# A fused ViT block: the slot experts in two batches, started four steps earlier, with constant products on TensorE

## The reference

```
p = patches(x)                          # 32 x 36 x 768
h = LN(LN(p) @ W_proj)                  # tokenizer, two layer norms with gains
q, k, v = h @ W_qkv ; q, k normalized over the tokens of an image
attn = softmax(q^T k * temp)            # per image and head, 24 x 24
h = LN(h + (attn v) @ W_proj + b_proj)
# slot experts: 8 experts x 4 slots
logits = unit(h) @ unit(slots) * scale  # per token 32 logits
D = softmax over tokens ; C = softmax over slots
X~ = D^T unit(h)                        # 32 slots x 192 per image
H  = gelu(X~[expert] @ W_down + b_down) # 24 values per slot
Y~ = H @ W_up[expert] + b_up            # 192 values per slot
h = LN(h + C Y~)
```

## Time and profile before

| | us |
|---|---|
| median of 3 runs | 141.82 (139.89 to 144.46) |
| profiled execution | 140.0 |
| its span | 138.0 |
| PE / DVE / ACT / POOL busy | 115.0 / 88.9 / 69.0 / 67.0 |
| mean granted TensorE clock | 0.939 |

### The profile page before, as it was taken

How to read it: one execution, slowest core, us unless ns; L and a number is a source line. 1 busy time by engine, 2 the same in 40 slices (tenths; PEclk the granted TensorE clock), 3 DMA queues, 4 the chain that set the end, 5 groups by cost and what they waited for, 6 DMA issues and landing times.

```text
span 138.0 us, 4819 instructions
## 1 busy us (share of the span) xinstructions
PE 115.0 (83%) x1779; PEld 93.6 (68%) x1779; DVE 88.9 (64%) x380; ACT 69.0 (50%) x234; POOL 67.0 (49%) x158
## 2 busy tenths in 40 slices
PE   0297799999699999999999999997986860999920
PEld 0297799888377868578787796866964630788700
DVE  0211999999643687985857558586987440159980
ACT  3000004242862848648675686846644468763553
POOL 8500277767847428837265382743664000007871
PEclk9999999999999999999999999999999555599995
DMA  1999899988000000000000000000000000000232
GB/s 14 337 293 278 269 305 320 314 319 214 5 7 0 5 0 7 5 0 7 0 5 5 0 5 0 10 5 0 5 0 7 0 0 0 5 0 24 72 89 71
DMA packets 7677, 10.34 MB, mean 75 GB/s; under 512 B 2056, under 2 KB 5032, under 8 KB 7656
## 3 DMA queue, kind: packets, MB, share of 16 engines
q1 hardware_dynamic: 7656, 10.06, 24.2%
HBM read 9.17 MB, written 0.88 MB: 73 GB/s over the span
## 4 chain that ended last, share of the span: by engine, by line
PE 47%; DVE 22%; issue 12%; POOL 10%; ACT 4%; DMA 3%; SPq 1%; POOLq 1%; DVEq 0%; ACTq 0%
DVE st L649 8%; PE ps L565 7%; PE ps L436 6%; PE ps L476 5%; PE ps L496 3%; PE ps L542 3%; PE ps L399 3%; DMA wt<-in_w_tok 3%; PE ps L489 3%; PE ps L519 3%; DVE y L663 3%; PE ps L578 3%; DVE st L671 2%; PE ps L507 2%; PE ps L407 2%
## 5 line engine op out<-in xcount | busy, mean ns | idle before, releaser
L417 PE MATMUL ps<-wc,xT 128*108 128x192 f32 (+1 forms) x132 | 23.0, 327 | 1.5 <-DVE wc L637 1.5
L940 ACT ACTIVATE hT<-ps,b,g 96x108 f32<-96x108 f32 (+1 forms) x22 | 8.4, 430 | 27.9 <-PE ps L426 27.9
L417 PEld LDWEIGHTS ps<-wc,xT 128*108 128x108 f32 (+1 forms) x132 | 20.7, 170 | 2.0 <-DVE wc L637 1.8
L436 PE MATMUL ps<-wqk,hT 96*108 96x384 f32 (+1 forms) x44 | 16.2, 490 | 0.7 <-ACT qp L962 0.7
L1125 POOL TENSOR_SCALAR pw<-mv 108x1 f32<-108x1 f32 (+1 forms) x11 | 3.7, 337 | 21.3 <-DVE mv L780 21.3
L476 PE MATMUL ps<-hT,wv 96*128 96x108 f32 (+1 forms) x88 | 12.5, 284 | 0.0
L1139 POOL TENSOR_SCALAR var<-mv 108x1 f32<-108x1 f32 (+1 forms) x11 | 2.4, 223 | 18.9 <-DVE mv L875 18.4
L950 ACT ACTIVATE sq<-ps 108x384 f32<-108x384 f32 (+1 forms) x11 | 5.4, 490 | 12.4 <-PE ps L436 12.4
L476 PEld LDWEIGHTS ps<-hT,wv 96*128 96x128 f32 x88 | 10.7, 191 | 0.7
L649 DVE BATCH_NORM_STATS2 st<-xs 108x6 f32<-108x384 f32 (+1 forms) x22 | 10.9, 540 | 0.2 <-issue 0.2
L960 ACT ACTIVATE km<-ps,imgsel 108x192 f32<-108x192 f32 (+1 forms) x32 | 11.0, 418 | 0.0
(11 more groups left out here) (106 smaller groups left out, 304.6 us busy)
## 6 DMA issues: line engine op xcount, KB each, us to landing
xT<-in_x_t SPq DMA_DIRECT2D x10, 324.0 KB, 7.0
xs<-in_x SPq DMA_DIRECT2D x10, 324.0 KB
out<-o SPq DMA_DIRECT2D x10, 81.0 KB
wt<-in_w_tok SPq DMA_DIRECT2D x1, 576.0 KB, 4.2
wqk<-in_w_qk SPq DMA_DIRECT2D x1, 288.0 KB, 8.7
xT<-in_x_t SPq DMA_DIRECT2D x1, 216.0 KB, 7.5
xs<-in_x SPq DMA_DIRECT2D x1, 216.0 KB
wv<-in_w_v SPq DMA_DIRECT2D x1, 192.0 KB, 9.0
```

The lines of the kernel that those rows point to most:

```text
L417: mm = pe.matmul(tokp(g), xT[:, o + kc * n:o + (kc + 1) * n], wc[:, kc, :], start=kc == 0, stop=kc == KC - 1)
L436: mm = pe.matmul(qkp(g), hT[:, f, t0:t0 + tokens(g)], wqk[:, f, :, :, :].rearrange("p j h d -> p (j h d)"), start=f == 0, stop=f == 1)
L940: ins = act.activation(hT[:, f, t0:t0 + tokens(g)], htp(g)[:, f, :], ACT.Identity, bias=b2[:, f:f + 1], scale=g2[:, f:f + 1])
```

## The change

- `hidden` works on two batches, groups 0 to 5 (18 images) and 6 to 10 (14 images). `w_down` and `w_up` are padded to 32 values per expert, so that each expert has 32 partitions, and pairs of experts lie side by side (`j = n // 2`). `gelu(b)` is two activations over all 128 partitions. `wu` comes in one load.
- In place of `slot_out`: `widen(b)` multiplies each expert's weights with its slots only, for the whole batch, 16 products that give the outputs with the 192 values on partitions (2 x 96) and the slots along the row; `take_lower` (ScalarE) and `take_upper` (VectorE) copy halves of them to SBUF; `turn_u(g)` turns a group back by the identity; `take_y(g)` copies it (ScalarE). The bias is a product of its own in `combine(g)`.
- hidden(0), gelu(0) and widen(0) run in step 12; turn_u and combine of groups 0 to 5 in steps 13 to 16 and behind them; the second batch after the last step.
- `keep_busy(count, bank)` multiplies a constant 128 x 128 tile with itself into a bank that is free then: 11 ahead of `offset`, 3 behind `column_means`, 2 in step 11, 3 or more in each step from 12 on, 9 around widen(1).

```diff
-HB = ((0, 4), (4, 8), (8, NG))
+HB = ((0, 6), (6, NG))
+HS = 12
+WIDE = {13: (0,), 14: (1, 2), 15: (3,), 16: (4, 5)}
...
-            sp.wait_ge(cleared, 6)
-            for j in range(4):
-                sp.dma_start(wu[32 * j:32 * j + HID, :, :], w_up[j]).then_inc(experts_in, 16)
+            sp.dma_start(wu[:, :, :].rearrange("p e d -> p (e d)"), w_up).then_inc(experts_in, 16)
...
+            def keep_busy(count, bank):
+                for _ in range(count):
+                    pe.matmul(ps[:, bank, 0:128], steady[:, :], steady[:, :], start=True, stop=True)
...
                 for n in range(NE):
-                    j = n % 4
+                    j = n // 2
                     for f in range(2):
-                        mm = pe.matmul(hp(b, i1 - i0)[32 * j:32 * j + HID, n // 4, :, :], wd[:, f, n, :],
+                        mm = pe.matmul(hp(b, i1 - i0)[32 * j:32 * j + 32, n % 2, :], wd[:, f, n, :],
                                        xt[:, f, i0:i1, n, :], start=f == 0, stop=f == 1,
                                        tile_position=(0, 32 * j))
...
+            def widen(b):
+                i0, i1 = batch(b)
+                pe.wait_ge(hb_ready, b + 1)
...
+                for e in range(2):
+                    for f in range(2):
+                        for j in range(4):
+                            r = slice(32 * j, 32 * j + 32)
+                            mm = pe.matmul(utp(i1 - i0)[:, j, f, :, e, :], wu[r, e, f * F:(f + 1) * F],
+                                           hb[r, e, 0:(i1 - i0) * NP], start=True, stop=True,
+                                           tile_position=(32 * j, 0))
+                mm.then_inc(utp_ready, 1)
...
+            def turn_u(g):
...
+                for f in range(2):
+                    u = widened(b)[:, f, i0:i0 + images(g), :, :]
+                    mm = pe.transpose(ytp(g)[:, f * F:(f + 1) * F],
+                                      u.rearrange("p i j s -> p (i j s)"), ident[0:F, 0:F])
+                mm.then_inc(ytp_ready, 1)
 
             def combine(g):
...
+                pe.matmul(yop(g), cT[0:sl, g, 0:n], bu[0:sl, :], start=True, stop=False)
+                pe.wait_ge(yt_ready, g + 1)
+                pe.matmul(yop(g), cT[0:sl, g, 0:n], yt[0:sl, g % NQ, :], start=False, stop=True).then_inc(yop_ready, 1)
+
+            pe.wait_ge(steady_set, 1)
+            keep_busy(11, 3)
             offset()
             column_means()
+            keep_busy(3, 3)
...
                 at(logits, s - 5)
+                if s == HS:
+                    pe.wait_ge(experts_in, 16 * (3 + 1))
+                    hidden(0)
...
                 at(mix, s - 2)
+                if s == HS - 1:
+                    keep_busy(2, 0)
+                if s == HS + 1:
+                    keep_busy(3, 5)
+                if s == HS + 2:
+                    keep_busy(3, 5)
+                if s > HS + 2:
+                    keep_busy(3, 5)
                 at(turn_xn, s - 4)
+                if s == HS:
+                    keep_busy(4, 2)
+                if s == HS + 2:
+                    keep_busy(3, 4)
                 at(slot_in, s - 6)
                 at(norms, s)
+                if s == HS:
+                    widen(0)
+                for g in wide(s - 1):
+                    combine(g)
+                for g in wide(s):
+                    turn_u(g)
+            combine(4)
+            hidden(1)
+            combine(5)
+            keep_busy(6, 5)
+            widen(1)
+            keep_busy(3, 5)
+            turn_u(6)
+            for g in range(7, NG):
+                turn_u(g)
+                combine(g - 1)
             combine(NG - 1)
```

(The waits of the keep_busy lines on the last reader of their bank are left out here.) VectorE does take_upper(0) at the end of step 12, and last_residual, last_stats and last_moments of the groups of `WIDE` one step after their turn_u, last_shift two steps after it; then take_upper(1) and groups 6 to 10. ScalarE:

```diff
             for s in range(17):
                 at(exp_e, s - 2)
                 at(take_v, s - 2)
+                if s == HS:
+                    act.wait_ge(experts_in, 16 * (3 + 1))
+                    gelu(0)
                 at(square, s)
                 at(take_c, s - 6)
...
                 at(exp_c, s - 5)
...
                 at(take_slots, s - 6)
-                if s == NG + 4:
-                    act.wait_ge(experts_in, 16 * (3 + 4))
-                    gelu(0)
+                if s == HS:
+                    take_lower(0)
+                for g in wide(s):
+                    take_y(g)
+                for g in wide(s - 3):
+                    last_norm(g)
+            last_norm(1)
+            last_norm(2)
             gelu(1)
-            gelu(2)
-            for g in range(NG):
+            take_lower(1)
+            take_y(6)
+            take_y(7)
+            last_norm(3)
+            take_y(8)
+            last_norm(4)
+            take_y(9)
+            last_norm(5)
+            take_y(10)
+            last_norm(6)
+            for g in range(7, NG):
                 last_norm(g)
```

More of the change, by code:

```diff
@@ L54, in at, with wide, batch @@
         stage(g)
+def wide(s):
+    return WIDE.get(s, ())
+def batch(b):
+    return HB[b][0] * GI, min(B, HB[b][1] * GI)
 def images(g):
@@ L557, in hidden @@
                 mm.then_inc(hp_ready, 1)
-            def slot_out(g):
-                i0, ni = g * GI, images(g)
-                pe.wait_ge(hb_ready, 1 + sum(g >= e for _, e in HB[:-1]))
+            def widen(b):
+                i0, i1 = batch(b)
+                pe.wait_ge(hb_ready, b + 1)
+                if b == 0:
+                    pe.wait_ge(v_ready, NG)
+                    pe.wait_ge(lnn_ready, NG)
+                    pe.wait_ge(e2_scaled, NG)
+                if b >= 1:
+                    pe.wait_ge(yt_ready, HB[b][0])
+                    pe.wait_ge(z2_ready, HB[b][0])
+                for e in range(2):
[6 more added lines that the diff above has]
+                mm.then_inc(utp_ready, 1)
@@ L562, in slot_out @@
+            def turn_u(g):
+                b = sum(g >= e for _, e in HB[:-1])
+                i0 = (g - HB[b][0]) * GI
+                pe.wait_ge(uT_lower, b + 1)
+                pe.wait_ge(uT_upper, b + 1)
                 if g >= 2:
                     pe.wait_ge(yt_ready, g - 1)
[L564 to L566 removed]
+                for f in range(2):
+                    u = widened(b)[:, f, i0:i0 + images(g), :, :]
+                    mm = pe.transpose(ytp(g)[:, f * F:(f + 1) * F],
+                                      u.rearrange("p i j s -> p (i j s)"), ident[0:F, 0:F])
@@ L894, in _ @@
             slot_sums()
-            for s in range(16):
+            for s in range(HS + 6):
                 if s == 4:
@@ L923, in _ @@
                 at(residual_moments, s - 2)
[L924 to L931, removed]
+                if s == HS:
+                    take_upper(0)
+                for g in wide(s - 1):
+                    last_residual(g)
+                for g in wide(s - 1):
+                    last_stats(g)
+                    last_moments(g)
+                for g in wide(s - 2):
+                    last_shift(g)
+            take_upper(1)
+            last_shift(4)
+            last_shift(5)
+            for g in range(6, NG + 1):
+                at(last_residual, g, 6)
+                at(last_stats, g, 6)
+                at(last_moments, g, 6)
+                at(last_shift, g - 1, 6)
         @block.scalar
@@ L1021, in gelu, with take_y, take_lower @@
             def gelu(b):
-                i0, i1 = HB[b][0] * GI, min(B, HB[b][1] * GI)
+                i0, i1 = batch(b)
                 act.wait_ge(hp_ready, b + 1)
[L1024 to L1027, removed]
-                ins.then_inc(hb_ready, 1)
+                if b >= 1:
+                    act.wait_ge(utp_ready, b)
+                for e in range(2):
+                    ins = act.activation(hb[:, e, 0:(i1 - i0) * NP], hp(b, i1 - i0)[:, e, :],
+                                         ACT.Gelu, bias=bd[:, e:e + 1])
+                ins.then_inc(hb_ready, 1)
+            def take_y(g):
+                s = images(g) * SL
+                act.wait_ge(ytp_ready, g + 1)
+                if g >= NQ:
+                    act.wait_ge(yop_ready, g - NQ + 1)
+                act.activation(yt[0:s, g % NQ, :], ytp(g), ACT.Copy).then_inc(yt_ready, 1)
+            def take_lower(b):
+                i0, i1 = batch(b)
+                act.wait_ge(utp_ready, b + 1)
+                if b >= 1:
+                    act.wait_ge(ytp_ready, HB[b][0])
+                act.activation(widened(b)[:, :, :, 0:2, :].rearrange("p f i j s -> p j (f i) s"),
+                               utp(i1 - i0)[:, 0:2, :, :, :, :].rearrange("p j f i e q -> p j (f i) (e q)"),
+                               ACT.Copy).then_inc(uT_lower, 1)
             def last_norm(g):
```

89 lines of the change are left out of this document (45 added, 44 removed).

## The result

The changed kernel takes 1.011 times the kernel before, 95% interval 1.006 to 1.016: medians of 7 runs each, 141.39 and 139.89 us. Forecast were 138.0 us and a gain. The profiled execution took 140.84 us with a span of 138.7, against 140.0 and 138.0. Either way no gain came. The ratios compare only the executions within 1.5% of the quickest of their kernel, the medians take all.

What follows compares the result with a forecast made beforehand. The prediction saw a chain of waits, VectorE early, then TensorE, engines in turn in steps 12 to 15, TensorE last. Terms +2.4, -3.1 and -1.2 gave a 136.0 us span, 138.0 with 2.0 around it; range 134.5 to 142.2.

Steps and rivals of the forecast that it cites:

- the head: Start of the kernel: constant products bring the weights 2.7 us earlier, late patch loads leave 1.2 us gained, ends 0 and 2.3.
- middle: TensorE's steady part, from the first turn_xn to mix(9): no change was forecast, 0.
- tail: From mix(9) to the end of the span: slot_in(10) starts 2.4 us later, the rest after it is 3.1 us shorter.
- lm(8): VectorE in the tail: slips behind exp_d(7), to start at 107.1 us instead of 103.75.
- xn(9): VectorE in the tail: take_upper(0) runs ahead of it, so it starts at 108.75 us instead of 104.56, +4.2.
- slot_in(10): TensorE, last steps: starts at 119.35 us instead of 116.99, +2.4; from there to the end 17.85 us for 20.96.
- widen: First batch, step 12: widen(0) takes 1.8 us, between bounds of 0.75 and 2.7.
- hidden: First batch, step 12: hidden(0), 32 records with 72 columns, takes 0.75 us to the start of the next.
- The table loads: ScalarE, step 12: two loads of 1.28 us around gelu(0) put exp_c(7) at 104.8 us instead of 101.0, +3.8.
- The falling clock: Rival: the clock still falls in the tail, some 3 us of half-clock work, 141.0 us, chance 0.25.
- a kind one for the kernel before: Profiled execution, 140.0 us: full clock came back just as TensorE was busy again, so it was held to favour the kernel before.
- the median, 141.82: Second reference, the median of three runs, 1.8 us above the profiled one; by it the forecast is 2.7% less.

Runs made afterwards that it cites:

- h1_light_order: Kernel before plus the 11 + 3 head products, rows of groups 4 to 10 loaded to a quarter width, later weights issued behind group 8's patches; ratio 0.979.
- e4: Changed kernel with Identity in place of Gelu in the first batch only, so only the second batch switches tables; ratio 0.990 to the kernel before.
- e3: Changed kernel without any constant product from step 11 on, the head's kept; ratio 1.065 to the kernel before.
- g3: Changed kernel without head products, with hidden's experts interleaved, Gelu table asked for early and fewer constant products in the tail; ratio 0.975 to the kernel before.
- g2: Kernel before with the rows of groups 4 to 10 loaded to a quarter of their width and no constant products; ratio 0.996.
- e5: Changed kernel with hidden's experts in the order 0, 2, 4, 6, 1, 3, 5, 7; ratio 0.989 to the kernel before.

## Why the prediction was wrong

**The step that failed is the head**: "I take the middle: 1.2 us gained". In the execution profiled the start of the steps came 1.66 us later; over all profiles it comes 0.27 us earlier, nothing of it is left at mix(9), and no timing with the full loads shows a gain beyond doubt. By parts, forecast and measured in that profile: head -1.2 and +1.66, middle 0 and +0.67, tail -0.75 (+2.4 and -3.1) and -1.57. The sum had its lower end at 0 and none below, because the effect was right (the weights 2.7 us early, VectorE idle before the reads of groups 3 and 4) but the bandwidth was taken from one execution as a constant. The same code reads group 9 at 33.53 in one execution and at 35.66 in another, and the kernel before was profiled in one with 34.01, the earliest of the six without head products: 1.3 us of luck in the reference's head, as large as the gain that was claimed. What the runs showed in its place: the head is bound by the queue. In the changed kernel's page the row DMA has the DMA engines 80% or more busy in slices 2 to 10 of 40 (3.47 us each), at 248 to 336 GB/s:

```profile
DMA  1999998889300000000000000000000000001122
GB/s 20 336 288 256 267 294 300 294 284 248 92 5 2 0 5 5 2 5 7 0 5 5 0 5 0 7 2 5 5 5 0 0 2 5 0 28 49 44 76 64
```

h1_light_order shows what that hides, with less to load and the weights behind: there all 2.7 us come through to VectorE's read of group 9, and 1.5 of them to the steps.

**Two terms were missing.** One is 0.1 to 0.7 us of TensorE pauses in the middle, in each of the twelve profiles with head products (39.21 to 39.76 us) and in none of the seven without (39.09 to 39.11, the kernel before among them). The trace puts them down to issue; no run shows them as stalls for instructions, as one expectation calls them, and what they wait for was not settled. The other is the granted clock behind the head, which falls to 0.50 in nine of the nineteen profiles and costs 0.1 to 1.3 us; seven of the nine have head products, of the ten without a fall five. The profiles of before and after have none, so it explains the averages and not the 1.66 us.

**The tail's way was right, its size by luck in part.** Shifted by the 2.33 us, lm(8) came at 107.36 (forecast 107.1), xn(9) at 108.83 (108.75), slot_in(10) at 118.65 (119.35), and from there to the end 17.73 us (17.85). So slot_in(10) came 1.66 us later than before and not 2.4, and the whole gave 1.57 for the 0.75 forecast. Inside it widen cost 0.84 and not 1.8, and hidden 1.46 and not 0.75: two errors that mostly cancel. That the order `j = n // 2` puts neighbours into one column group stood in the diff and was not priced.

**The table loads** were counted one to one on the path. exp_c(7) did come 4.3 us later, 3.8 forecast, but e4 shows that TensorE's queue stood there too.

**The rivals.** The falling clock was given 0.25 and 3 us; it did not come, and e3 shows that its price was 10, for the clock did not return: the 3 us counted on its return as in the earlier trace rows. Some 1.2 to 2.2 us of the tail's gain by profile are missing in the timing; the forecast took the tail of one profile, 41.15 us, for the tail of every execution. It called this execution "a kind one for the kernel before"; its head was (34.01), its tail was the unkind one, with 13.6 us at the low clock where h1 had 6.8. And of its two references the median, 141.82, was the wrong one: the later medians of the kernel before are 139.9 to 141.1, so the 2.7% by it was never there.

## What to carry to other kernels

Where an engine's head start runs into transfers, price it by the bytes that the queue must deliver by then, with the spread of several executions, before counting any of it. Where the clock falls, one profile is not the kernel: compare the mean granted clock of all timed executions with that of the profiled one before taking its low stretch for a price. Constant products are worth testing alone first: here the restructuring that they came with loses 6% without them and gives nothing with them, until its issue order and its table loads are put right. When small products share the array by column group, write the loop so that the group changes from one expert to the next (0.68 us for 32 records here, against 1.46), and ask for an activation table ahead of the wait, not behind it (in g3 the load of 1.28 us lies in the wait for hidden(0)).

## What the runs showed of the hardware

- The clock fell with no pause of TensorE over 0.77 us from 94 us up to it (0.77 at 96.27 in the kernel before, 0.68 at 106.25 in e3). By stretch, the kernel before and then e3, up to the fall:

```profile
94.00:107.50 13.50, 10.75 (x196) 8.67 (x195) 11.53 (x63) 6.76 (x31) 6.47 (x15) 1.00 0.01 3
```

```profile
94.00:107.50 13.50, 11.82 (x299) 10.36 (x296) 8.98 (x47) 8.83 (x29) 7.04 (x16) 0.99 0.01 4
```

- Nor does it come back at the first busy stretch: in e3 it stayed at 0.50 from 109 to 145 us, with 3.00 of 3 busy at 121 and 4.00 of 4 at 136, where before it came back at the end of one such stretch.
- The same steps had the clock at 0.50 for 13.6, 10.2 and 6.8 us in different executions (before, g2, h1).
- It also fell to 0.50 between 34 and 46 us, behind the head, in nine of nineteen profiles; from the read of group 9 to the first turn_xn it then took 23.83 to 25.04 us, in the other ten 23.67 to 23.72.
- 32 records of 72 columns on 32-column tiles took 0.68 us to the next record when the column group changed every four records (e5) and 1.46 us when it changed every eight (the changed kernel).
- A table load can be placed in a wait (1.28 us at 101.07 in g3).
- 28 more records at the head go with pauses of TensorE in the middle, up to 0.58 us each (in twelve of twelve profiles with them, in none of seven without); why is not known.
